# First attention layer: the causal mask of the exponential scores moves from a TensorE product to a GpSimd select, and the probabilities wait one quad longer

## The reference

```python
def _L0_attn_ref(hidden_states, w_attn, b_attn, w_proj, b_proj):
    qkv = hidden_states @ w_attn.T + b_attn
    ...
    w = jnp.einsum('bhnd,bhmd->bhnm', q, k) * jax.lax.rsqrt(float(D))
    mask = jnp.tril(jnp.ones((S, S), dtype=jnp.float32))
    w = jnp.where(mask > 0, w, NEG)
    w = jax.nn.softmax(w, axis=-1)
    attn = jnp.einsum('bhnm,bhmd->bhnd', w, v)
    attn = attn.transpose(0, 2, 1, 3).reshape(B, S, E)
    return attn @ w_proj.T + b_proj
...
x = L0_attn_hidden_states
x = x + _L0_attn_ref(_layernorm(x, axis=-1), ...)
x = x + _L0_ffn_ref(_layernorm(x, axis=-1), ...)
x = x + _L1_attn_ref(_layernorm(x, axis=-1), ...)
x = x + _L1_ffn_ref(_layernorm(x, axis=-1), ...)
```

## Time and profile before

| what | value |
|---|---|
| median of 3 runs | 2297.63 us (2297.55 to 2308.24) |
| profiled execution | 2295.53 us, span 2293.8 us |
| PE, DVE, ACT, POOL busy over the span | 87%, 69%, 61%, 47% |
| first layer | from about 60 to 860 us of the span |

### The profile page before, as it was taken

The page is one execution under the profiler, slowest core; times in us unless marked ns, Lnnn a source line. Parts: engine busy times, 40 slices in busy tenths (PEclk is TensorE's granted clock), DMA queues, the critical chain, the costliest instruction groups (busy, mean ns, idle before and its releaser), DMA issues.

```text
span 2293.8 us, 45190 instructions
## 1 busy us (share of the span) xinstructions
PE 1985.7 (87%) x13603; PEld 994.7 (43%) x13603; DVE 1588.6 (69%) x4202; ACT 1396.3 (61%) x3097; POOL 1078.2 (47%) x1777
## 2 busy tenths in 40 slices
PE   2999999999999939999828889999999999899984
PEld 1455455554455419989701223333333333333333
DVE  3888888887888633332126788888888887888844
ACT  0466666666666624444305677777777777777772
POOL 6433746547455250000064565666656665664222
PEclk7899999999999969999957999999999999999997
DMA  6232223223232024444312222222222122221100
GB/s 176 79 96 68 86 75 89 76 73 92 69 92 78 24 67 144 142 136 139 108 57 72 65 62 61 65 62 61 61 65 69 57 60 65 62 61 49 54 6 14
DMA packets 167648, 174.15 MB, mean 76 GB/s; under 512 B 42544, under 2 KB 126192, under 8 KB 167280
## 3 DMA queue, kind: packets, MB, share of 16 engines
q1 hardware_dynamic: 157776, 153.87, 22.7%
q0 software_dynamic: 8192, 16.79, 2.6%
q10 hardware_dynamic: 1440, 0.60, 0.1%
HBM read 120.30 MB, written 49.28 MB: 74 GB/s over the span
## 4 chain that ended last, share of the span: by engine, by line
PE 23%; DVE 15%; issue 5%; SPq 3%; ACT 2%; POOL 2%; DMA 1%; ACTq 0%; DVEq 0%; POOLq 0%
DVE l_rowmax L1818 8%; PE bank L1604 6%; PE bank L1592 5%; PE pair L1581 3%; SPq L78 2%; PE bank L1678 2%; PE bank L1651 2%; PE pair L1658 2%; DVE l_hq L236 2%; PE bank L1618 1%; DVE l_stats L1854 1%; DVE l_hq L259 1%; POOL l_chosen_rows L1404 1%; SPq L98 1%; PE bank L1668 1%
## 5 line engine op out<-in xcount | busy, mean ns | idle before, releaser
L1818 DVE TENSOR_REDUCE l_rowmax<-pair 128x2 f32<-128x1024 f32 x512 | 597.0, 1216 | 145.7 <-PE pair L1581 145.5
L1727 ACT ACTIVATE l_probs<-bank 128x512 f32<-128x512 f32 x1024 | 554.1, 602 | 95.4 <-PE bank L1592 90.1
L907 DVE CUSTOM_DVE_ANT_0 pair<-pair,mask_rows_q 128x512 f32<-128x512 f32 (+3 forms) x1024 | 476.0, 517 | 98.3 <-PE pair L667 91.7
L823 ACT ACTIVATE l_probs<-bank 128x256 f32<-128x256 f32 (+3 forms) x769 | 307.6, 444 | 107.8 <-PE bank L679 104.6
L1592 PE MATMUL bank<-q_stack,k_stack 128*128 128x512 bf16 x1024 | 321.0, 389 | 26.2 <-DMA q_stack<-l_rowmaxT 13.6
L667 PE MATMUL pair<-k_stack,q_stack 96*128 96x512 bf16 (+3 forms) x1024 | 315.2, 313 | 25.2 <-DVE l_rowmax L907 14.9
L1604 PE MATMUL bank<-l_probs,v_aug 128*32 128x512 f32 x2048 | 276.7, 612 | 2.6 <-ACT l_oT L1772 2.6
L1581 PE MATMUL pair<-k_stack,q_stack 64*128 64x512 bf16 x1024 | 177.6, 394 | 93.3 <-DVE l_rowmax L1818 63.6
L677 PE MATMUL bank<-q_stack,k_stack 128*128 128x256 bf16 (+3 forms) x769 | 231.8, 306 | 0.2
L691 PE MATMUL bank<-l_probs,v_aug 128*32 128x512 f32 (+3 forms) x2048 | 192.2, 448 | 20.3 <-ACT l_probs L823 17.7
L1592 PEld LDWEIGHTS bank<-q_stack,k_stack 128*128 128x128 bf16 x1024 | 74.9, 97 | 253.0 <-ACT l_probs L1727 135.1
(11 more groups left out here) (286 smaller groups left out, 3383.2 us busy)
## 6 DMA issues: line engine op xcount, KB each, us to landing
q_stack<-scratch SPq DMA_DIRECT2D x192, 96.0 KB
k_stack<-scratch SPq DMA_DIRECT2D x192, 96.0 KB
experts_w<-in_w SPq DMA_DIRECT2D x72, 256.0 KB, 2.5
q_stack<-scratch SPq DMA_DIRECT2D x320, 48.0 KB
k_stack<-scratch SPq DMA_DIRECT2D x320, 48.0 KB
scratch<-l_q_parts SPq DMA_DIRECT2D x32, 384.0 KB, 2.5
scratch<-l_k_parts SPq DMA_DIRECT2D x32, 384.0 KB, 2.6
experts_rows<-rows_in SPq DMA_DIRECT2D x72, 128.0 KB, 2.2
```

The lines of the kernel that those rows point to most:

```text
L823: nc.scalar.activation(probs[:, (a * HG + j) % PSLOTS, c0:S], bank[:, c0:S], ACT.Exp, scale=SCALE).then_inc(t_read, 1)
L907: nc.vector.tensor_tensor_reduce(scores, scores, m["mask_rows_q"][:, S - keys(t):S], 1.0, LOWEST, ALU.add, ALU.max, rowmax[:, g % 2, c:c + ...
L1727: nc.scalar.activation(probs[:, (a * HG + j) % PSLOTS, :], bank[:, :], ACT.Exp, scale=SCALE).then_inc(t_read, 1)
L1818: nc.vector.tensor_reduce(largest, banks[:, :].rearrange("p (k n) -> p k n", k=2), X_AXIS, ALU.max).then_inc(s_read, 1)
```

## The change

Four parts, all in the first layer but for the last.

1. The product with `mask_rows_k` is gone from `scores_for_exp`, 1024 of them. ACT exponentiates unmasked scores. POOL then sets the probabilities of later keys to zero in `drop_later_keys`: one `affine_select` over the four heads' diagonal blocks of a quad, [128, 4, 128] f32. `probs_v` waits for it (`causal`) and no longer for ACT.
2. `probs_v` (and the copy `take_out` of a finished group) come one slot later, two behind the exponentials (`LAG`); `probs` has twelve slots in place of eight.
3. On POOL, the two `split` tasks are cut into halves, `split_high` and `split_low`, in slots 3 and 4 for q and 5 and 6 for k.
4. `b2` is allocated and loaded in the experts' stage and `passed` shares the memory of `probs`.

```diff
@@ -162,8 +158,6 @@
                 sp.dma_start(m["x"][:, b, :].rearrange("p (t e) -> p t e", t=TT),
                              dram["x"][b].rearrange("(t p) e -> p t e", p=P)).then_inc(m["x_loaded"][min(b, 2)], 16)
 
-            b2 = dram["b2"]
-            sp.dma_start(m["b2"][:, :, :], bass.AP(b2.tensor, b2.offset, [[0, P], [E, NE], [1, E]])).then_inc(m["experts_loaded"], 16)
             sp.dma_start(m["w2"][:, :, :, :], dram["w2"].rearrange("p (e c) d -> p e c d", e=NE)
                          ).then_inc(m["experts_loaded"], 16)
 
...
@@ -366,6 +360,8 @@
     scratch = dram["scratch"]
     LN = 7
     F = 12
+    LAG = 2
+    SLOTS0 = (LAG + 1) * HG
     NJ, region, CH = expert_tiles(NB), routed_rows(NB), NB * TT * 2
 
     WIDTH = {b: 2 if b < NB - 2 else 1 for b in range(NB) if b % 2 or b >= NB - 2}
...
@@ -381,7 +377,7 @@
     DVE_WORK = [("stats", 0, -24), ("stats2", 0, F + 22), ("best", 0, F + 32), ("which", 0, F + 33), ("chosen", 0, F + 34),
                 ("find", 0, F + 36), ("before", 0, F + 37), ("shares", 0, F + 38)]
     POOL_WORK = [("split_max", g, 4 * g + 4) for g in range(G)]
-    POOL_WORK += [("factors", 0, -23), ("normalise", 0, -21), ("split", 0, -13), ("split", 1, -11), ("bias", 0, -9),
+    POOL_WORK += [("factors", 0, -23), ("normalise", 0, -21), ("split_high", 0, -13), ("split_low", 0, -12), ("split_high", 1, -11), ("split_low", 1, -10), ("bias", 0, -9),
                   ("factors2", 0, F + 24)] + [("scatter", k, F + 40 + k) for k in range(2 * 2 * TT)]
     SP_WORK = [("max_out", g, 4 * g + 7) for g in range(G)] + [("parts", 0, -11), ("parts", 1, -9)]
     SP_WORK += [("stack", g, (-7, -4, 0, 4)[g]) for g in range(G)]
...
@@ -400,7 +396,7 @@
         sem = lambda name: mem.sem("l0_" + name)
 
         q_stack, k_stack, v_aug = m["q_stack"], m["k_stack"], m["v_aug"]
-        probs = sb("probs", [P, PSLOTS, S])
+        probs = sb("probs", [P, SLOTS0, S])
         stats, mean_var, rstd = sb("stats", [P, TT, 6]), sb("mean_var", [P, TT, 2]), sb("rstd", [P, 4, TT])
         xn, xnT = sb("xn", [P, TT, E]), sb("xnT", [P, S])
         qk_f = [sb("q_f", [P, S]), sb("k_f", [P, S])]
...
@@ -568,10 +565,22 @@
                 nc.gpsimd.tensor_scalar(parts[:, 0, :], f[:, :], 1.0, 0.0, ALU.mult, ALU.add).then_inc(split_step, 1)
                 pool.wait_ge(split_step, base + 1)
                 nc.gpsimd.tensor_tensor(f[:, :], f[:, :], parts[:, 0, :], ALU.subtract).then_inc(split_step, 1)
+
+            def split_low(b, which):
+                f, parts = qk_f[which], qk_parts[which]
+                base = 8 * b + 4 * which
                 pool.wait_ge(split_step, base + 2)
                 nc.gpsimd.tensor_scalar(parts[:, 1, :], f[:, :], 1.0, 0.0, ALU.mult, ALU.add).then_inc(split_step, 1)
                 pool.wait_ge(split_step, base + 3)
                 nc.gpsimd.tensor_tensor(parts[:, 2, :], f[:, :], parts[:, 1, :], ALU.subtract).then_inc(split_step, 1)
+
+            def drop_later_keys(a):
+
+                t = a % TT
+                pool.wait_ge(t_read, at[("exp", a, HG - 1)] + 1)
+                diagonal = probs[:, a * HG % SLOTS0:a * HG % SLOTS0 + HG, first(t):first(t) + P]
+                nc.gpsimd.affine_select(out=diagonal, in_=diagonal, compare_op=ALU.is_ge, fill=0.0, base=0,
+                                        pattern=[[0, HG], [1, P]], channel_multiplier=-1).then_inc(causal, 1)
 
             def split_max(b, g):
                 n = b * G + g
...
@@ -620,6 +629,8 @@
             for s in slots:
                 if s == 0:
                     constants()
+                if uses.exp_quad(s - 1) is not None:
+                    drop_later_keys(uses.exp_quad(s - 1))
                 for kind, b, k in due(POOL_WORK, s):
                     if kind == "split_max":
                         split_max(b, k)
...
@@ -675,21 +688,19 @@
                     pe.wait_ge(max_rows, 16 * PARTS * (b * G + g + 1))
                 bank = t_bank(("exp", a, j))
                 nc.tensor.matmul(bank[:, first(t):S], k_stack[b % 2][:, h_, t * P:(t + 1) * P],
-                                 q_stack[b % 2][:, h_, first(t):S], start=True, stop=False)
-                nc.tensor.matmul(bank[:, first(t):first(t) + P], ident_bf[:, :], m["mask_rows_k"][:, :],
-                                 start=False, stop=True).then_inc(t_mm, 1)
+                                 q_stack[b % 2][:, h_, first(t):S], start=True, stop=True).then_inc(t_mm, 1)
 
             def probs_v(a):
                 b, quad = divmod(a, QUADS)
                 g, t = divmod(quad, TT)
-                pe.wait_ge(t_read, at[("exp", a, HG - 1)] + 1)
+                pe.wait_ge(causal, a + 1)
                 if quad == 0:
                     pe.wait_ge(s_read, at[("v", b, 0)] + 1)
                 if t == 0 and a > 0:
                     pe.wait_ge(oT_ready, b * G + g)
                 for j in range(HG):
                     last = nc.tensor.matmul(pv_bank[j * VW:(j + 1) * VW, first(t):S], v_aug[b % 2][:, t, g * HG + j, :],
-                                            probs[:, (a * HG + j) % PSLOTS, first(t):S], start=t == 0, stop=t == TT - 1)
+                                            probs[:, (a * HG + j) % SLOTS0, first(t):S], start=t == 0, stop=t == TT - 1)
                 last.then_inc(pv_done, 1)
 
             def turned_rows(b):
...
@@ -777,8 +788,8 @@
                 e, a = uses.exp_quad(s), uses.max_quad(s)
                 for j in range(HG):
                     if j == HG // 2:
-                        if uses.exp_quad(s - 1) is not None:
-                            probs_v(uses.exp_quad(s - 1))
+                        if uses.exp_quad(s - LAG) is not None:
+                            probs_v(uses.exp_quad(s - LAG))
                         for kind, b, k in due(MIDDLE, s):
                             if kind == "xnT":
                                 turned_rows(b)
...
@@ -818,9 +829,9 @@
             def exp(a, j):
                 bank = written(("exp", a, j))
                 c0 = first(a % TT)
-                if a >= 2:
-                    act.wait_ge(pv_done, a - 1)
-                nc.scalar.activation(probs[:, (a * HG + j) % PSLOTS, c0:S], bank[:, c0:S], ACT.Exp, scale=SCALE).then_inc(t_read, 1)
+                if a > LAG:
+                    act.wait_ge(pv_done, a - LAG)
+                nc.scalar.activation(probs[:, (a * HG + j) % SLOTS0, c0:S], bank[:, c0:S], ACT.Exp, scale=SCALE).then_inc(t_read, 1)
 
             def read(kind, b, k):
                 bank = written((kind, b, k))
...
@@ -875,8 +886,8 @@
                         for kind, b, k in due(MIDDLE, s):
                             if RING[kind] == "t":
                                 read(kind, b, k)
-                    if j == HG - 1 and uses.exp_quad(s - 1) is not None and uses.exp_quad(s - 1) % TT == TT - 1:
-                        take_out(*divmod(uses.exp_quad(s - 1) // TT, G))
+                    if j == HG - 1 and uses.exp_quad(s - LAG) is not None and uses.exp_quad(s - LAG) % TT == TT - 1:
+                        take_out(*divmod(uses.exp_quad(s - LAG) // TT, G))
                     if uses.exp_quad(s) is not None:
                         exp(uses.exp_quad(s), j)
                 for kind, b, k in due(END, s):
...
@@ -1148,8 +1160,10 @@
                 sp.wait_ge(y_ready, j + 1)
                 sp.dma_start(dram["rows_out"][j].rearrange("(s p) e -> p s e", p=P), y[k][:, :, :]).then_inc(stored[k], 16)
 
-            for j in range(3):
-                load(j)
+            load(0)
+            sp.dma_start(b2[:, :, :], bass.AP(dram["b2"].tensor, dram["b2"].offset, [[0, P], [E, NE], [1, E]])).then_inc(b2_loaded, 16)
+            load(1)
+            load(2)
             for slot_, rows_, width, src in weights4:
                 sp.dma_start(w4[0:rows_, slot_, 0:width], src).then_inc(fp4_loaded, 16)
             for j in range(NJ + 1):
...
@@ -1222,7 +1236,7 @@
 
         @block.vector
         def _(dve):
-            dve.wait_ge(m["experts_loaded"], 32)
+            dve.wait_ge(b2_loaded, 16)
 
             def quantise_weights(k, part):
 
```

More of the change, by code:

```diff
@@ L133, in _ @@
                                     fill=MASKED, base=0, pattern=[[-1, P]], channel_multiplier=1).then_inc(set_, 1)
[L135 to L136 removed]
             for i in range(2):
                 nc.gpsimd.memset(m["v_aug"][i][:, :, :, :], 0.0).then_inc(set_, 1)
[L140 removed]
+            pool.wait_ge(set_, 11)
             for i in range(2):
                 nc.gpsimd.memset(m["v_aug"][i][:, :, :, D:D + 1], 1.0).then_inc(set_, 1)
[L143 removed]
+            pool.wait_ge(set_, 13)
             zero(nc.gpsimd, m["k_stack"][1], k_cleared[1])
@@ L560, in normalise, with split_high @@
                 nc.gpsimd.tensor_tensor(xn[:, :, :], xn[:, :, :], along_rows(rstd[:, 1, :]), ALU.mult).then_inc(xn_ready, 1)
-            def split(b, which):
+            def split_high(b, which):
                 f, parts = qk_f[which], qk_parts[which]
@@ L629, in _ @@
```

(6 more changed lines are left out.)

28 lines of the change are left out of this document (12 added, 16 removed).

## The result

| | before | after |
|---|---|---|
| median | 2297.59 us (2292.82 to 2308.24, 4 runs) | 2346.36 us (2345.89 to 2347.15, 4 runs) |
| profiled span | 2293.8 us | 2345.4 us |

The account below looks back on a forecast made before the run. PE was busiest, with PE and DVE holding each other up by turns. Groups -44, scatter batches +38, drain +2 gave -4 us on 2295.5, so 2291.5; the forecast median was 2294 us, no change, range 2266 to 2324.

Parts of the forecast that it names:

- The select's price: Each of 256 selects on POOL in the first layer: 0.64 us, bounds 0.29 and 1.16.
- The rival of dear selects: Slots 4 to 13 of scatter batches: selects at 1.16 us make stalls cost 66 us, 2322 us in all; chance 0.17.
- Scatter batches: PE waits for POOL's select between slots 4 and 13: 7.2 us in each of five, 2 in the sixth, 38 us.
- 16 x 0.64 = 10 us more leave it room: Plain batches: 10 us of selects beside POOL's 19.6 us leave it room, so no stall was counted.
- I take 1.1 us for a group: PE's gain in each of 35 free groups, with 0.4 us in 14 others: 44 us; bounds 20 and 60.
- The two together: First layer: 44 us gained in groups against 38 us lost in scatter batches, two large effects that nearly cancel.
- the gain doesn't come: First-layer groups gain only 0.5 us because DVE is last more often: +20 us, 2318 us; chance 0.07.
- The distance of one more slot: Between exponential and values: PE's 40.4 us wait for ACT should go, about 0.6 us a group.
- The drain: End of the first layer: the last scatters wait for the last exponentials and delay the last routing, costing 2 us.
- The rival of the clock: Scatter batches' stalls each bring two more dips of PE's clock: 16 us, 2310 us in all; chance 0.06.

Follow-up runs that it names:

- e17: Kernel after without its selects, so the second pass is unmasked; two-slot distance and twelve slots kept. Ratio 0.9896 to the kernel before.
- e9: Kernel after with POOL's k split, bias and second normalisation's factors one slot later, q split unmoved. Ratio 1.018 to the kernel before.
- e16: Kernel after with each of the 256 selects covering one head's block instead of four, waits unchanged. Ratio 1.0114 to the kernel before.
- e11: Kernel after without its selects, with four banks for the first pass and three for the second, not three and four. Ratio 0.9804 to the kernel before.
- e1: Kernel after with the mask product put back and no select, leaving the two-slot distance and twelve slots. Ratio 1.0023 to the kernel before.
- e2: Kernel before without the mask product and nothing in its place, at the old distance and banks. Ratio 0.994 to the kernel before.
- e12: Kernel before without the mask product, with four banks for the first pass and three for the second, not three and four. Ratio 0.9808.
- e7: Kernel before with four banks for the first pass and three for the second, not three and four; nothing else. Ratio 0.9859 to the kernel before.
- e3: Kernel after without its selects, second pass unmasked, on a chip where the kernel before took 2359 us. Ratio 0.9932 to the kernel before.

## Why the prediction was wrong

- **The select's price** was right: 0.64 us predicted, 0.638 measured. The rival of dear selects falls with it.
- **Scatter batches** were right, in size and in mechanism: 7.2 us of stall each for five, 2 for the sixth, 38 in all, from 34.5 us of POOL's list, which took 34.9 (with one wait of 1.1 us for DVE in it, so that the last 0.4 is chance). Against e17, batches 4, 6, 8, 10 and 12 are longer by 7.1 us on average (52.9 - 45.7) and batch 14 by 5.6 (49.67 - 44.09): 41 us.
- **"16 x 0.64 = 10 us more leave it room"** is the step that failed. I took the batch's sum for plain batches, where I had looked at the single slots for scatter batches. A select has a deadline of its own each, and the lump of slots 3 to 5 lies across one of them. Against e17 the other batches from 1 to 15 lose 32 us, predicted zero. A plain batch loses 3.0 us before the product of slot 4's quad, 1.1 before slot 5's, 0.4 each before those of slots 6 and 14, and nothing before the rest. The first is the wait for the select, which e9 takes away whole by moving POOL's work behind it, and e16 in part; in the batch shown above the second is the lower clock behind that wait.
- **"I take 1.1 us for a group"** was mis-sized: 44 us of gain predicted. Between the first product with the values and the last but one, before took 733.0 us, e17 708.9, after 785.3: the gain was 24 us, and the selects cost 76 (41 + 32 + 3 in the last batch). Where the gain went stands in the waits: those for DVE's three banks rose from 28.2 to 108.1 us. I named DVE as the cap, by its work of 38 to 40 us a batch. e11 shows that this work was not yet the limit: with a bank more, DVE does it in a batch 3 us shorter. That three banks run dry while PE multiplies with the values fits these waits, but is not shown by itself, and a fourth bank let no more of the mask product's time through, since other waits took its place. What caps a group's gain in the end stays open.
- **The two together**: for the layer I had -44 + 38 = -6 us, and it was 52 longer. Of these 58 us, 35 are the selects' cost in batches where I had put it at nothing, 20 the gain that didn't come, and 3 the scatter batches.
- **The rival "the gain doesn't come"**, given 0.07, was nearest by its mechanism: 2318, with a loss of 20 us from 0.5 a group. It explains one of the two large errors; the plain batches' loss was in none of the cases, so that the range ended at 2324.
- **The distance of one more slot** was to give about 0.6 us a group; e1 shows nothing (1.0023). PE's wait for ACT before the values went from 40.4 to 8.6 us there, and its wait for DVE's banks from 28.2 to 54.4.
- **The drain** was right: from the last product with the values to the first of the experts' stage it is 42.4 us before (857.73 - 815.36) and 44.4 after (911.90 - 867.55), 2.0 us more. POOL began the last batch's factors 8.3 us behind the last product before, and 10.1 after, behind its last scatter. `b2` cost nothing that shows: from there to the end of the span it is 1436.1 us before and 1433.5 after.
- **The clock** stood at nothing in my sum, and it has a part in the loss. Between the first product with the values and the last but one it was at its lower level for 21 us in the kernel before, for 10 in e17 and for 61 in the kernel after, in six, three and sixteen stretches. At half speed for 51 us more than e17, PE loses 26 us at most of the 76. How much of it really comes through is not separated, since POOL's list sets the pace in part of these stretches. The lower clock came with the waits for the selects, which e17 doesn't have. The rival of the clock, given 0.06, had twelve stretches more and 16 us; there were ten more. By itself it is much too small for the result.

## What to carry to other kernels

When an operation is moved onto an engine with a mixed list, compare not busy sums but each instance with its deadline: add up what stands ahead of it in that engine's list since its input came, and look where the lumps lie. Count what a stall does to TensorE's clock behind it, too. And before counting a saving on one of two engines that hold each other up, look at the waits that will take its place: 56 us of mask products gave 14 us with three banks in DVE's ring (e2) and 12 with four (e12 against e7). The depth of that ring, one number, was worth 1.4% by itself.

## What the runs showed of the hardware

A GpSimd `affine_select` over four blocks of 128 columns, 2 KB apart in each partition, took 0.638 us (0.624 to 0.672), one block of them 0.294: 0.115 us for each 128 further columns. No run has the four blocks side by side, so what the stride costs is not shown; a one-input operation on 512 columns in a row took 0.622 us. The Trainium skill, GPSIMD Engine Reference, section Key points, has GpSimd contend with VectorE for the SBUF interfaces that they share, where VectorE's instruction is in a 2-port mode or has two SBUF inputs. Over 256 selects, none took longer than 0.672 us, so the select shows no such slowing in this layer.

TensorE's granted clock fell behind waits of PE: after one of 2.94 us it was 0.50 for the next 3 us, and eight matmuls that take 1.07 us at 1.00 took 1.93.

The same program took 2343.7 us on one chip (e3) and 2269.6 on another (e17), with the same busy time of POOL (1076.2 and 1078.1 us) and the same median of a scatter's issue (0.965 and 0.966 us). Near the end of the first layer in e3 PE stood still behind nothing that the profile shows, where e17 has no such row:

```profile
812.84 0.39 PE L688 MATMUL bank<-q_stack,k_stack 128*128 128x256 bf16 x1 [6.54 <-issue]
```

What it waits for there stays open, and this row is a small part of the difference between the chips. That difference is the reason for comparing ratios, and why scatter batches of one chip (48.5 in e3) aren't set against those of another (45.7 in e17).
